# Cross attention with a routed expert layer: scores_T and products with V in pairs of units, and a reordered tail

## The reference, cut to what matters

```python
# x (8, 112, 256), ctx (8, 375, 192); 16 heads of 16; 8 experts, 112 places each
xn = layernorm(x)
q, k, v = xn @ Wq + bq, ctx @ Wk + bk, ctx @ Wv + bv          # per head
attn = softmax(einsum('bhqd,bhkd->bhqk', q, k) * 0.25)
x = x + tanh(g_xattn) * (einsum('bhqk,bhkd->bhqd', attn, v) @ Wo + bo)
t = layernorm(x).reshape(896, 256)
probs = softmax(t @ wg); e = argmax(probs)                      # one expert per token
place = number of earlier tokens with the same e; kept where place < 112
x = x + tanh(g_ffn) * gate * (t @ W[e].T + b[e])                # zero where not kept
```

## Time and profile before

| | us |
|---|---|
| median of 3 runs (203.81 to 206.55) | 206.45 |
| profiled execution | 201.78 |
| its span, first to last instruction | 200.0 |
| PE busy, share of the span | 179.3 (90%) |
| DVE / ACT / POOL busy | 126.7 / 97.0 / 95.1 |

### The profile page before, as it was taken

One profiled execution on the slowest core, in us unless ns is written; L12 is line 12 of the kernel. 1 busy time (PEld: TensorE's weight loads), 2 busy tenths in 40 slices (PEclk: granted clock), 3 DMA queues, 4 the chain that ended last, 5 costly groups with the idle time before them and its releaser, 6 DMA issues.

```text
span 200.0 us, 4484 instructions
## 1 busy us (share of the span) xinstructions
PE 179.3 (90%) x1723; PEld 104.9 (52%) x1723; DVE 126.7 (63%) x301; ACT 97.0 (49%) x215; POOL 95.1 (48%) x159
## 2 busy tenths in 40 slices
PE   1998795699999999999999999998998957989991
PEld 1456554356556466566556546655565633347640
DVE  6398775846485486567658548668804624678752
ACT  4846554336564573684566457375557630022200
POOL 6686976902290573456169057342070372102750
PEclk9999999789999999999999999999999997999998
DMA  5985898591259149428965901914630054921220
GB/s 167 272 194 131 215 236 217 130 256 26 54 146 202 51 120 248 132 79 197 242 162 131 211 4 53 223 65 151 190 97 3 0 162 128 290 67 30 78 60 23
DMA packets 19886, 27.22 MB, mean 136 GB/s; under 512 B 4000, under 2 KB 14857, under 8 KB 19752
## 3 DMA queue, kind: packets, MB, share of 16 engines
q1 hardware_dynamic: 17253, 23.76, 47.8%
q0 software_dynamic: 864, 2.07, 3.4%
q10 hardware_dynamic: 1747, 1.09, 1.9%
HBM read 10.03 MB, written 5.06 MB: 75 GB/s over the span
## 4 chain that ended last, share of the span: by engine, by line
PE 73%; DVE 10%; DMA 4%; POOL 3%; issue 3%; SPq 2%; another core or an unknown queue 2%; ACT 1%; DVEq 0%; POOLq 0%
PE pv L554 15%; PE stp L538 13%; PE sc L526 10%; PE pj L473 5%; PE misc L589 4%; PE pj L495 3%; PE pj L478 3%; DMA q<-parts_q 2%; DVE nmax L986 2%; PE pj L500 2%; PE pj L642 2%; PE misc L676 2%; PE stp L456 2%; DMA wk_sb<-in_wk 2%; PE sc L642 2%
## 5 line engine op out<-in xcount | busy, mean ns | idle before, releaser
L986 DVE TENSOR_REDUCE nmax<-sc 112x1 f32<-112x375 f32 x128 | 67.3, 544 | 35.4 <-PE sc L526 34.3
L888 ACT ACTIVATE prob<-stp 128x448 f32<-128x448 f32 (+1 forms) x96 | 52.3, 544 | 48.6 <-PE stp L538 45.3
L526 PE MATMUL sc<-k,q 128*112 128x375 bf16 x128 | 40.6, 342 | 6.1 <-DVE nmax L986 2.9
L554 PE MATMUL pv<-prob,v_sb 128*32 128x112 f32 (+1 forms) x768 | 38.4, 271 | 3.0 <-issue 2.4
L538 PE MATMUL stp<-q,k 128*128 128x112 bf16 x384 | 36.0, 217 | 0.0
L538 PEld LDWEIGHTS stp<-q,k 128*128 128x128 bf16 x384 | 21.0, 99 | 16.4 <-issue 16.4
L554 PEld LDWEIGHTS pv<-prob,v_sb 128*32 128x32 f32 (+1 forms) x768 | 15.3, 108 | 23.9 <-issue 15.2
L526 PEld LDWEIGHTS sc<-k,q 128*112 128x112 bf16 x128 | 16.0, 131 | 14.7 <-DVE nmax L986 9.5
L1249 POOL CAST mparts<-nmax 112x16 bf16<-112x16 f32 x8 | 1.6, 196 | 40.7 <-DVE nmax L986 40.7
L473 PE MATMUL pj<-ctx_sb,wk_sb 128*128 128x375 f32 x32 | 15.4, 580 | 4.5 <-DMA wk_sb<-in_wk 4.5
L1233 POOL TENSOR_TENSOR kf<-kf,parts_k 128x375 f32<-128x375 f32 x14 | 12.6, 897 | 11.6 <-ACT kf L787 11.5
(11 more groups left out here) (151 smaller groups left out, 265.5 us busy)
## 6 DMA issues: line engine op xcount, KB each, us to landing
k<-parts_k SPq DMA_DIRECT2D x42, 187.5 KB, 3.8
ctx_sb<-in_ctx SPq DMA_DIRECT2D x7, 375.0 KB, 3.3
early<-in_wT SPq DMA_DIRECT2D x8, 256.0 KB, 4.9
slots<-empty SPq DMA_DIRECT2D x8, 224.9 KB, 5.0
ctx_sb<-slots SPq DMA_DIRECT2D x8, 224.9 KB, 4.5
q<-parts_q SPq DMA_DIRECT2D x12, 112.0 KB, 3.4
k<-parts_k SPq DMA_DIRECT2D x12, 93.8 KB, 2.5
q<-parts_q SPq DMA_DIRECT2D x6, 168.0 KB, 4.3
```

The costliest lines, as they stand in the source:

```text
L526: pe.matmul(sc[n % 2][0:NQ, 0:NK], q_heads(b)[:, h, :], k6_flat[:, b % KR, h * NK:(h + 1) * NK], start=True, stop=True).then_inc(s_sc, 1)
L554: mm = pe.matmul(pv[32 * j:32 * j + 32, g * NQ:(g + 1) * NQ], v_sb[0:kn, b % VR, v_block(c, 4 * g + j), :], prob[0:kn, n % 3, j * NQ:(j + ...
L888: nc.scalar.activation(prob[0:kn, n % 3, :], stp[n % 2][0:kn, 0:4 * NQ], ACT.Exp, scale=SCALE).then_inc(s_p, 1)
L986: nc.vector.tensor_reduce(nmax[:, b % 2, h:h + 1], sc[n % 2][0:NQ, 0:NK], axis=AX.X, op=ALU.max, negate=True).then_inc(s_max, 1)
```

## The change

`units_at` replaces `at` for `scores_T`, the exponentials and `probs_v`: for batches 0 to 6 the even slot of a batch's units issues two units and the odd one none; batch 7 keeps one per slot. `HEADS` doubles slots 2, 4, 8, 9 and no longer 2, 3, 4, 11. `turn_pv` and `divide` move one slot earlier. In the tail: the dense products use four banks; two of tile 7's come ahead of the experts; POOL's scatters leave the loop, wait for the end of all products with V, and the sixth comes behind `rstd_2(7)`.

```diff
-HEADS = ((0,), (1,), (2, 3), (4, 5), (6, 7), (8,), (9,), (10,), (11,), (12,), (13,), (14, 15))
+HEADS = ((0,), (1,), (2, 3), (4,), (5, 6), (7,), (8,), (9,), (10, 11), (12, 13), (14,), (15,))
-NORM_AT, WO_AT, ADD_AT = (30, 31, 32), 33, 34
+NORM_AT, WO_AT, ADD_AT = (29, 30, 32), 33, 34
-SCAT_AT = (108, 109, 110, 111, 112, 113)
+def units_at(s, offset):
+    if not (found := at(s, offset)):
+        return []
+    b, n = found
+    if b == B - 1:
+        return [(b, n)]
+    return [(b, n), (b, n + 1)] if n % 2 == 0 else []
...
-                if (found := at(s, T_AT)):
+                for found in units_at(s, T_AT):
                     scores_T(*found)
...
-                if found := at(s, PV_AT):
+                for found in units_at(s, PV_AT):
                     probs_v(*found)
             pe.wait_ge(s_wT, 16 * E)
             dense(0, 0)
             places(1, GATHERED, GATHERED + 1)
+            dense(0, 1)
             through_wo(B - 1)
+            dense(0, 2)
             turn_share(0)
-            dense(0, 1)
-            dense(0, 2)
+            dense(0, 3)
+            choose_bias(0)
             turn_xn2(B - 1)
-            choose_bias(0)
             logits(B - 1)
-            dense(0, 3)
+            dense(1, 0)
+            dense(1, 1)
             places(2, B - 1, B)
...
             product(E - 1)
-            pe.wait_ge(s_beTe, 2)
-            pe.wait_ge(s_res, E - 1)
-            for p in range(4):
-                dense(1, p)
+            dense(1, 2)
+            dense(1, 3)
...
-                if s in SCAT_AT:
-                    if s == SCAT_AT[0]:
-                        pool.wait_ge(s_cleared, 16 * E)
-                        pool.wait_ge(s_slot, 1)
-                    scatter(SCAT_AT.index(s))
-            rstd_2(B - 1)
+            pool.wait_ge(s_cleared, 16 * E)
+            pool.wait_ge(s_slot, 1)
+            pool.wait_ge(s_pv, B)
+            for b in range(GATHERED):
+                scatter(b)
+                if b == GATHERED - 2:
+                    rstd_2(B - 1)
```

More of the change, by code:

```diff
@@ L628, in dense @@
             def dense(t, p):
[L630 to L635, removed]
+                n = 4 * t + p
+                if n == 3:
+                    pe.wait_ge(s_pvt, B)
+                if 4 <= n < 7:
+                    pe.wait_ge(s_densed, p + 1)
+                if n == 7:
+                    for i, bank in enumerate(pj):
+                        pe.wait_ge(s_densed, 5 + i)
                         for c in range(2):
                             mm = pe.matmul(bank[0:NQ, 0:D], x2T[:, (GATHERED + t) % 2, c, :],
-                                           wT_sb[:, 2 * p + n, c, :], start=(c == 0), stop=(c == 1))
+                                           wT_sb[:, 2 * p + i, c, :], start=(c == 0), stop=(c == 1))
                         mm.then_inc(s_dense, 1)
@@ L883, in _ @@
             for s in range(END):
-                if found := at(s, T_AT):
-                    b, n = found
+                for b, n in units_at(s, T_AT):
                     kn = CHUNKS[n % NCH][1]
@@ L1052, in count @@
                 before_me = sc[1][0:NQ, 0:(hi - lo) * E].rearrange("p (b e) -> p b e", e=E)
[L1053 to L1058, removed]
+                link(nc.vector.tensor_tensor(own[:, lo:hi, :], before_me, maskb[:, lo:hi, :], ALU.mult))
                 link(nc.vector.tensor_reduce(place[:, lo:hi], own[:, lo:hi, :], axis=AX.X, op=ALU.add))
@@ L1082, in take_bias @@
                 dve.wait_ge(s_beT, t + 1)
-                nc.vector.tensor_tensor(last[:, t, :], (stp, sc)[t][1][0:NQ, 0:D],
-                                        (last[:, t, :], rows[:, GATHERED + t, X1:X1 + D])[t], ALU.add)\
-                    .then_inc(s_beTe, 1)
+                nc.vector.tensor_tensor(last[:, t, :], bias_bank[t], last[:, t, :], ALU.add).then_inc(s_beTe, 1)
                 dve.wait_ge(s_beTe, t + 1)
             def add_dense(t, p):
[L1089 to L1096, removed]
-                    dve.wait_ge(s_dense, 9)
[L1098 to L1102, removed]
+                n = 4 * t + p
+                one, two = dense_bank[p][0:NQ, 0:D], dense_bank[p][0:NQ, D:2 * D]
+                if n == 7:
+                    one, two = (bank[0:NQ, 0:D] for bank in pj)
+                dve.wait_ge(s_dense, n + 1)
+                link(nc.vector.scalar_tensor_tensor(last[:, t, :], one, share[:, t, 2 * p:2 * p + 1],
+                                                    last[:, t, :] if p else rows[:, GATHERED + t, X1:X1 + D],
+                                                    ALU.mult, ALU.add))
+                if n == 7:
+                    dve.wait_ge(s_dense, 9)
+                nc.vector.scalar_tensor_tensor(last[:, t, :], two, share[:, t, 2 * p + 1:2 * p + 2],
+                                               last[:, t, :], ALU.mult, ALU.add).then_inc(s_densed, 1)
+                dve.wait_ge(s_densed, n + 1)
             zero_q = q6[:, :].bitcast(F32)
@@ L1127, in _ @@
             for s in range(END):
-                if found := at(s, NORM_AT[0], 1):
+                if (found := at(s, NORM_AT[0], 1)) and found[0] < B - 1:
                     turn_pv(found[0])
@@ L1193, in _ @@
                     take_bias(1)
-            for p in range(4):
-                add_dense(1, p)
+            add_dense(1, 2)
+            add_dense(1, 3)
         @block.gpsimd
```

28 lines of the change are left out of this document (16 added, 12 removed).

## The result

The changed kernel takes 196.78 us (median of 6 runs, 195.27 to 200.98) against 205.88 (median of 6, 203.22 to 206.55) for the kernel before, run in turn on the same chip: ratio 0.9613, 95% interval 0.9526 to 0.9701. The ratio compares fast runs alone (within 1.5% of the fastest of the same kernel), while the medians are of all runs, whose ratio would be 0.956. That is faster; the forecast was 195.2, range 190.5 to 202.5. Its profiled execution took 196.03, with a span of 194.3, against 201.78 and 200.0.

What follows compares the result with a forecast made beforehand. PE, busy 90% of the span, was taken as the bound, with layout changes costing 0.09 a side. Slots -5.2, scatters -4.9 and tail +0.3 took 201.78 to 192.0; 3.2 for timed runs gave 195.2, range 190.5 to 202.5.

Steps and rivals of the forecast that it cites:

- Pairs: Batches 0 to 6: each of 42 pairs saves one PE layout change in and one out, 0.18, together 7.6 less.
- the rival built on it: Pairs save nothing because the second unit's weight loads wait for the first's streams: 201.9 us, chance 0.20.
- turn_pv at zero: `turn_pv` a slot sooner costs nothing, covered by slot 5 and 6 work; without cover 0.4 once a batch.
- Heads' waits: Slots 3 and 4: head 6's score waits 0.36 for a maximum instead of 0.15, 0.2 x 6 = 1.2 more.
- K's laying: Batch 3's first score waits 0.65 for K's transfers, as PE's slots get shorter; 0.9 taken for five batches.
- the +0.6 for slots 85/86 and 91/92: Late slots without K or V work: a pair costs 1.9 where two slots cost 1.6, 2 x 0.3 more.
- The start: Up to batch 1's first scores_T: -0.3 for the start, -1.1 for six pairs, +0.2 for a heads' wait.
- Late signals: Last exponential 1.7 and `turn_pv` 3.2 late while scatters run; issuing no scatter before them gains 4.9.
- The tail: From `turn_pv` to the last output: dense products move ahead of a wait but other chains grow as much, +0.3.
- P: The start of `turn_pv` in the tail, from which the forecast counts the later steps.
- late signals return: Rival: PE signals come late again under the moved scatters behind `turn_pv`, +5.1, 200.3 us, chance 0.22.
- 3.2 of the excess: Timed runs lay 2.0 to 4.8 above the profiled one, median 4.7; 3.2 carried over, from 192.0 to 195.2.

Runs made afterwards that it cites:

- Pairs alone: The kernel before with units in pairs and nothing else, old heads, `turn_pv` place and tail: 200.82 us, ratio 1.0105, 17.25 a batch.
- chip B: Chip of one of the three follow-up series; the kernel before has a median of 203.66 there, the change run again 196.26, ratio 0.962.
- the kernel with the scatters first: The changed kernel with all six scatters ahead of `rstd_2(7)`, where the sixth came behind it: 195.76 us, ratio 0.9495.
- the one before with waiting scatters: The kernel before with one wait more, POOL's first scatter waiting for the end of all products with V: 202.36 us, ratio 1.02.
- chip A: Chip of one of the three follow-up series; the kernel before has a median of 199.11 there.
- chip C: Chip of one of the three follow-up series; the kernel before has a median of 206.38 there.
- the change's slots: The kernel before with pairs, the new heads and `turn_pv` a slot sooner, old tail: 196.99 us, ratio 0.9833, 16.00 a batch.
- the tail alone: The changed kernel with one unit a slot and the old heads and `turn_pv` places, only the tail changed: 200.6 us against 199.11 for the kernel before.
- heads apart and keep busy: The changed kernel with a doubled heads slot moved from slot 4 to 0 and nine extra PE products at slot 12: 196.93 us, ratio 0.9569.
- both kernels on chip B with scatters under the last units: The change with its scatters back in the loop, 198.32 us; and the kernel before with pairs and `turn_pv` sooner, old heads and tail, 203.21 us.
- the two such kernels on chip A: The kernel before with pairs only, 200.82 us; and with pairs, new heads and `turn_pv` sooner, old tail, 196.99 us.

## Why the prediction was right, and where not

**Pairs** (-0.18 each). Right in kind, a little small. Products of two units take 0.09 + 0.52 where two single ones took 2 x 0.42, scores_T 0.40 where it was 2 x 0.21: 0.24 to 0.25 saved, 1.45 a batch. Four passes follow one another by less than 0.13, so the second unit's loads don't wait. The Trainium skill, "TensorE: Matmul & The Clock Gate", Step-by-step, lets weight loads go ahead where row groups don't conflict or the load goes to the background buffer; the trace shows no wait in a pair (16 products from 89.36 to 89.88), so the rival built on it (201.9) is refuted.

**turn_pv at zero** holds as a term of this sum: in the changed kernel PE nowhere waits for `turn_pv` (in the kernel before once, 0.5). What I had not seen is that the move is what makes the pairs pay. In the new order the old place costs 0.75 a batch, more than the slots' whole gain of 0.65. Pairs alone are slower than before by 0.60 a batch. I had looked at what stands behind `turn_pv`, not at the maximum ahead of it on DVE's list, and not at what the old place costs in the new order.

**Heads' waits** (+0.2 a batch) are the slots' term that I got wrong, right in place and too small: of 1.45 saved by pairs, 0.65 is left, so waits of 0.8 remain. Summed from start to next start on PE between the first scores_T of batches 4 and 5, the 16 scores take 3.98 where they took 3.35, and the logits 0.49 where they took 0.40. (My sum for head 6 is off too: 0.42, 0.36 and 0.54 make 1.32, not 1.38.) The score in slot 4 waits 0.29, and scores wait for maxima for 12.4 + 3.8 in all, where it was 9.5 + 2.9. The new heads were not just neutral: the old ones with pairs cost 0.5 a batch more.

**K's laying** (+0.9) didn't come. Batch 3's first score, at 66.33, starts 0.68 after the last landing (65.65). From the first of the six transfers to that score it is 8.71, before 9.08: 0.37 less, not 0.95. And the last landing comes 8.03 after the first issue, where it took 8.91: I had read the end of the row, 61.13, as the last issue, but the sixth transfer starts at 59.61 and lands at 65.20. Nor did the +0.6 for slots 85/86 and 91/92 come: from batch 6's first scores_T to batch 7's it is 13.93 before and 13.13 after, 0.80 less, more than a full batch gains. So the slots from batch 1 on come out at -4.1 where the sum has -4.0, but by errors that cancel: pairs save more than I took, waits for maxima cost more, and two costs were not there. That agreement is luck.

**The start** (-1.2) went the other way, +1.8, mostly by clock. I had put a clock loss, up to 1.7 a place, inside the range and not into the sum. How much is lost there is not fixed by the order: the change itself shows half clock for 10.2 in its first profile and for 6.8 on chip B, the kernel with the scatters first none. Two kernels show the start without half clock: the one before with waiting scatters (chip A), which has the old order there, and the one with the scatters first (chip C), which has the new. Their clock lines:

```profile
PEclk9999999999999999999999999999999999969998
...
PEclk9999999999999999999999999999999999999999
```

Batch 1's first scores_T stands at 55.55 in the one and at 55.07 in the other, so the new order gains 0.5 there where the clock takes nothing, in its direction right and less than the 1.2. The rest of the +1.8 comes with half clock, 10.2 in place of 3.4.

**Late signals** (-4.9) were right: -4.8, and 4.9 between the two kernels on chip B. But it is no law: on chip A they never came. There the change's slots gave 0.983 and its tail nothing; the whole change was not run there.

**The tail** (+0.3). The steps hold within 0.6: the last `res` ends at P + 25.8 (forecast 25.3), the read issued at P + 11.45 (10.9), PE's last expert product ended at P + 24.9 (24.9). What wasn't in the sum is the last add, 1.26 late. Take it away and P to the end is 32.4, forecast 32.5; in the two kernels with this tail whose last add was on time (the tail alone, and heads apart and keep busy) it is 32.6 and 32.8. It is the rival "late signals return", in a place that I hadn't named: the change moved the last dense products under the output's scatters. They were 0.5 to 2.7 late in seven of the eight kernels with that tail on chips B, C and the first one, 0.1 in the eighth (heads apart and keep busy, though its last product too ends just ahead of the last scatter); 0.1 in the one on chip A; and 0.1 in all five with the old tail, where the last product ends 2.5 after the last scatter. So the rows go together with the scatters but don't prove them to be the cause; no kernel was run that moves only that.

**From execution to median.** I carried 3.2 of the excess; the changed kernel's median is 0.75 above its profiled execution. That error (2.5) and those above (4.1) are of opposite sign, so 195.2 lies nearer to 196.78 than the steps deserve: that too is luck.

## What to carry to other kernels

When work is grouped so that PE changes its array layout less often, the saving (here 0.24 a pair) is only the first half of the sum: for each bank and each pair, look up which instruction of another engine now stands ahead of the one that frees it, and move that too, since here the grouping alone was a loss (17.25 a batch in place of 16.65). Price each companion edit against the new order, not against the old one: in the old order PE waited for `turn_pv` 0.5 in all, so its place looked like nothing. And a wait taken away tends to uncover the one it covered (0.29 for a maximum, then 0.60 for a copy), so cost the next one before you move heads.

## What the hardware showed that was not expected

- Signals of PE arrived up to 3.4 us behind the end of the product while POOL's indirect transfers ran, on some chips and not on others: by 1.7 (exponential) and 3.2 to 3.4 (`turn_pv`) in the profile before and in both kernels on chip B with scatters under the last units, and not at all in the two such kernels on chip A.
- In one and the same order around 31 to 45 us, half clock lasted from 0 to 10.2 us, behind a gap of 1.66 to 2.31 us in which PE waited for q, and the length of the gap did not tell which (1.65 with 10.2 of half clock in one kernel, 1.66 with none in another). Nine extra products in that gap took 1.3% and 1.1% off the medians, on two chips.
